# Pair slots of a ViT block: second norm folded behind two transposes, one lag more for ranks and scatters

## What is computed

```python
xn = _layernorm(x, norm1_w, norm1_b)
qkv = (xn @ qkv_w.T + qkv_b)...                  # 12 heads of 16
attn = softmax(q @ k.T * scale); o = attn @ v
x = x + (o @ proj_w.T + proj_b)
xn2 = _layernorm(x, norm2_w, norm2_b)            # the second norm
logits = xn2 @ w_gate                            # 8 experts
top_vals, top_idx = top_k(logits, 2); gates = softmax(top_vals)
h = gelu(xn2 @ W1[e] + b1[e])                    # 768 wide, for the token's two experts
x + sum over e of gate_e * (h @ W2[e] + b2[e])
```

## Time and profile before

| | us |
|---|---|
| median of 3 runs | 1150.55 (1149.22 to 1151.24) |
| the profiled execution | 1158.98 |
| its span | 1157.1 |
| PE, DVE, ACT, POOL busy in the span | 998.3, 636.4, 466.9, 565.4 |
| pair slots | about 484 to 835 |
| expert tiles | about 852 to 1112 |

### The profile page before, as it was taken

The page is one execution under the profiler, slowest core; times in us unless marked ns, Lnnn a source line. Parts: engine busy times, 40 slices in busy tenths (PEclk is TensorE's granted clock), DMA queues, the critical chain, the costliest instruction groups (busy, mean ns, idle before and its releaser), DMA issues.

```text
span 1157.1 us, 24046 instructions
## 1 busy us (share of the span) xinstructions
PE 998.3 (86%) x6992; PEld 854.6 (74%) x6993; DVE 636.4 (55%) x1649; ACT 466.9 (40%) x1172; POOL 565.4 (49%) x1094
## 2 busy tenths in 40 slices
PE   7899999999997987599888888888349999999960
PEld 4789889889975654488677776766339999999950
DVE  7477585575437787466667666665412222222216
ACT  1234323233213444345565555555114444444424
POOL 2578586676421223414666666666504444434330
PEclk9989999999988998799899999998569999999985
DMA  8564662470103300306200000000011111111118
GB/s 356 205 266 189 225 275 95 190 306 34 39 11 62 63 1 0 58 1 266 105 13 16 16 16 16 16 16 19 26 48 38 41 43 43 36 43 42 44 35 253
DMA packets 41701, 103.09 MB, mean 89 GB/s; under 512 B 7046, under 2 KB 28656, under 8 KB 38837
## 3 DMA queue, kind: packets, MB, share of 16 engines
q1 hardware_dynamic: 30085, 88.86, 22.1%
q0 software_dynamic: 5760, 9.68, 2.5%
q10 hardware_dynamic: 5808, 3.96, 1.1%
HBM read 86.30 MB, written 18.32 MB: 90 GB/s over the span
## 4 chain that ended last, share of the span: by engine, by line
PE 35%; POOLq 22%; issue 21%; POOL 7%; DVE 6%; DMA 4%; ACT 2%; DVEq 1%; SPq 1%; ACTq 0%
PE pe L1631 16%; POOLq L561 6%; POOLq L537 4%; PE pe L1640 4%; POOLq L526 2%; DMA x<-yy_d 2%; POOL xn L532 1%; POOLq L539 1%; POOLq L510 1%; POOLq L551 1%; POOL xs_d L529 1%; DVE sc L316 1%; PE pe L183 1%; DMA raw<-in_xw 1%; PE pe L184 1%
## 5 line engine op out<-in xcount | busy, mean ns | idle before, releaser
L1631 PE MATMUL pe<-wm,xm 128*128 128x193 f32 x1008 | 174.1, 331 | 1.7 <-issue 1.7
L1631 PEld LDWEIGHTS pe<-wm,xm 128*128 128x128 f32 x1008 | 168.0, 192 | 6.4 <-issue 6.4
L844 ACT ACTIVATE hT<-pe,eb 128x128 f32<-128x128 f32 x336 | 92.8, 375 | 147.6 <-PE pe L970 147.5
L983 PE MATMUL pp<-w2s,hT 128*128 x672 | 118.5, 326 | 0.0
L983 PEld LDWEIGHTS pp<-w2s,hT 128*128 128x128 f32 x672 | 107.9, 190 | 0.2
L967 PE MATMUL pe<-xsT,ew 128*128 128x128 f32 x672 | 89.4, 284 | 3.3 <-ACT xsT L834 3.3
L967 PEld LDWEIGHTS pe<-xsT,ew 128*128 128x128 f32 x672 | 81.1, 195 | 8.6 <-ACT xsT L834 4.1
L759 DVE TENSOR_TENSOR ys<-pp,b2s 128x192 f32<-128x192 f32 x56 | 20.0, 358 | 121.4 <-PE pp L983 118.5
L529 POOL DMA_INDIRECT xs_d<-xsrc,dst x64 | 65.6, 1025 | 41.7 <-issue 41.7
L557 POOL DMA_INDIRECT yy_d<-ys,yix x56 | 57.2, 1022 | 46.5 <-issue 46.5
L1355 POOL TENSOR_TENSOR sqs<-sqs,sqt 128x448 f32<-128x448 f32 x56 | 67.5, 1205 | 8.0
(11 more groups left out here) (267 smaller groups left out, 2220.3 us busy)
## 6 DMA issues: line engine op xcount, KB each, us to landing
xm<-in_xm SPq DMA_DIRECT2D x7, 2688.0 KB, 14.0
raw<-in_xwa SPq DMA_DIRECT2D x7, 1792.0 KB, 7.2
raw<-in_xwb SPq DMA_DIRECT2D x7, 1536.0 KB, 11.4
x<-in_x SPq DMA_DIRECT2D x4, 1536.0 KB, 8.6
xs<-xs_d SPq DMA_DIRECT2D x56, 96.5 KB
x<-yy_d SPq DMA_DIRECT2D x8, 672.0 KB
w1s<-in_W SPq DMA_DIRECT2D x1, 4608.0 KB
w2s<-in_W SPq DMA_DIRECT2D x1, 4608.0 KB
```

What stands on the lines that cost most here:

```text
L844: last = f(self.hT[:, u, c], pe1[:, 2 * u + c % 2, (c // 2) * ROWS:(c // 2 + 1) * ROWS], ACT.Gelu, bias=self.b1[:, u, c:c + 1])
L983: last = mm(pp[:, u, 0:D], self.hT[:, u, n], self.w2s[:, bass.ds(e, 1), n * D:(n + 1) * D].rearrange("p o d -> p (o d)"), start=(n == 0), ...
L1631: mm(y[:, 0:D + 1], cell(q, c), wm[:, q, c], start=(q + c == 0), stop=(q == 3 and c == KC - 1))
```

## The change

The second norm's weight and bias leave POOL. They are now per-partition columns: `colg` gets two more columns for the gate logits, and `n2` becomes a 128x2x2 tile for the expert tiles. They are applied by ACT where it copies transposed data out of PSUM: `xnT2` in the pair slots and `xsT` in the expert tiles, each now two Identity instructions of 128 columns (one for each half of the 192 numbers) with a scale column and a bias column, where one plain copy of 256 columns stood. POOL keeps the two statistics columns of every pair in a new tile `rn` (one more drain and copy), so that ACT can write `xsrc` two slots later from `x2`. Ranks go from lag 6 to 7, `xsrc` from 5 to 7, the scatter from 7 to 8 (40 POOL slots in place of 39), and POOL's slot ends with a drain. The values' products go to a bank of `pp`, so that the scores no longer wait for `on`. On DVE the first norm's statistics come first in a slot; the order on PE and ACT is changed as well.

```diff
-        self.n2 = sb("n2", [P, 2, D])
+        self.n2 = sb("n2", [P, 2, 2])
+        self.rn = sb("rn", [P, NP, 2])
...
-            a, b, c, d = item(0), item(4), item(3), item(7)
+            a, c, d = item(0), item(3), item(8)
...
-            if b:
-                pool.wait_ge(self.c_x, b[0] + 1)
-                g.tensor_tensor(self.xn[:, b[1]], self.xn[:, b[1]], self.n2[:, 0], ALU.mult)
             if d:
                 i, u, _ = d
-                pool.wait_ge(self.d_src, i + 2)
+                pool.wait_ge(self.d_src, i + 1)
                 pool.wait_ge(self.d_dst, i + 1)
...
-            pool.drain()
-            if d:
+                pool.drain()
                 for k in range(2):
...
-            if b:
-                g.tensor_tensor(self.xn[:, b[1]], self.xn[:, b[1]], self.n2[:, 1], ALU.add).then_inc(self.c_xn, 1)
...
-                g.tensor_scalar(st[:, 9:10], st[:, 6:7], st[:, 8:9], -1.0, ALU.mult, ALU.mult).then_inc(self.c_r, 1)
+                g.tensor_scalar(st[:, 9:10], st[:, 6:7], st[:, 8:9], -1.0, ALU.mult, ALU.mult)
+                pool.drain()
+                g.tensor_copy(self.rn[:, bass.ds(i, 1), :].rearrange("p o k -> p (o k)"), st[:, 8:10]).then_inc(self.c_r, 1)
...
-        run_slots(pool, NP, 8, slot)
+            pool.drain()
+        run_slots(pool, NP, 9, slot)
...
-            f(self.xsT[:], pt1[:, u, 0:2 * ROWS].rearrange("p (h n) -> p h n", h=2), ACT.Copy).then_inc(self.e_xT, 1)
+            for h in range(2):
+                last = f(self.xsT[:, h], pt1[:, u, h * ROWS:(h + 1) * ROWS], ACT.Identity, bias=self.n2[:, h, 1:2], scale=self.n2[:, h, 0:1])
+            last.then_inc(self.e_xT, 1)
...
+            if n7 is not None:
+                u, h = item(7)[1:]
+                act.wait_ge(self.scat[u], 32 * h)
+                f(self.xsrc[:, u, :, 0:D], self.x2[:, bass.ds(n7, 1), :].to_broadcast([P, 2, D]), ACT.Identity, bias=col(n7, 1), scale=col(n7, 0)).then_inc(self.d_src, 1)
...
-                pe.wait_ge(self.b_on, n2)
...
-                            last = mm(pe1[m * B:(m + 1) * B, 0, n * w:(n + 1) * w], self.pT[:, n, m * B:(m + 1) * B], self.vbd[:, m, n], start=True, stop=True)
+                            last = mm(pp[m * B:(m + 1) * B, 1, 256 + n * w:256 + (n + 1) * w], self.pT[:, n, m * B:(m + 1) * B], self.vbd[:, m, n], start=True, stop=True)
```

More of the change, by code:

```diff
@@ L607, in slot @@
         def slot(item):
-            n0, n1, n2, n3, n6 = (item(lag) and item(lag)[0] for lag in (0, 1, 2, 3, 6))
+            n0, n1, n2, n3, n6, n7 = (item(lag) and item(lag)[0] for lag in (0, 1, 2, 3, 6, 7))
             lg = self.lg
             dve.drain()
+            if n0 is not None:
+                v.bn_stats(self.bn[:, 0], row(hall, n0))
             if n6 is not None:
@@ L617, in slot @@
                 v.tensor_copy(lg[:], pe1[:, 3, 256:256 + E]).then_inc(self.d_lgo, 1)
+            dve.drain()
             if n0 is not None:
-                v.bn_stats(self.bn[:, 0], row(hall, n0))
-            dve.drain()
+                v.bn_aggr(st[:, 0:2], self.bn[:, 0]).then_inc(self.a_var, 1)
             if n2 is not None:
@@ L669, in slot @@
                 v.reciprocal(self.mx2[:], o[:, :, AHD:AHD + 1].rearrange("p h o -> p (h o)"))
-            dve.drain()
-            if n2 is not None:
+                dve.drain()
                 dve.wait_ge(self.c_T, n2)
@@ L776, in scalar, with row, col @@
         act.wait_ge(self.init, 2)
+        def row(t, i):
+            return t[:, bass.ds(i, 1), :].rearrange("p o d -> p (o d)")
+        def col(i, k):
+            return self.rn[:, bass.ds(i, 1), k:k + 1].rearrange("p o k -> p (o k)")
         def slot(item):
-            n0, n1, n2, n3, n4, n5, n6 = (item(lag) and item(lag)[0] for lag in (0, 1, 2, 3, 4, 5, 6))
+            n0, n1, n2, n3, n4, n5, n6, n7 = (item(lag) and item(lag)[0] for lag in (0, 1, 2, 3, 4, 5, 6, 7))
+            if n2 is not None:
+                act.wait_ge(self.b_sub, n2 + 1)
+                f(self.pm[:, :, 0:T], self.pm[:, :, 0:T], ACT.Exp, scale=AHD ** -0.5).then_inc(self.b_ex, 1)
+            if n5 is not None:
+                act.wait_ge(self.c_nT, n5 + 1)
+                for h in range(2):
+                    last = f(self.xnT2[0:H2, h], pe1[0:H2, 3, h * P:(h + 1) * P], ACT.Identity, bias=colg[:, h, 6:7], scale=colg[:, h, 5:6])
+                last.then_inc(self.d_out, 1)
             if n3 is not None:
@@ L804, in slot @@
                 f(self.xh2[:], self.x2[:, bass.ds(n0, 1), :].rearrange("p o d -> p (o d)"), ACT.Copy, scale=self.st[:, 3:4]).then_inc(self.a_xh, 1)
+            if n4 is not None:
+                act.wait_ge(self.c_r, n4 + 1)
+                f(self.xn[:, item(4)[1]], row(self.x2, n4), ACT.Identity, bias=col(n4, 1), scale=col(n4, 0)).then_inc(self.c_x, 1)
+            if n0 is not None:
                 act.wait_ge(self.a_T, n0 + 1)
@@ L872, in slot @@
         def slot(item):
-            n0, n1, n2, n3, n5, n6 = (item(lag) and item(lag)[0] for lag in (0, 1, 2, 3, 5, 6))
+            n0, n1, n2, n3, n5, n7 = (item(lag) and item(lag)[0] for lag in (0, 1, 2, 3, 5, 7))
             if n2 is not None:
@@ L924, in slot @@
                     last.then_inc(self.b_pT, 1)
-            if n5 is not None:
-                pe.wait_ge(self.d_out, n5 + 1)
-                for h in range(2):
-                    last = mm(pe1[:, 3, 256:256 + E], self.xnT2[:, h], self.wgate[:, h], start=(h == 0), stop=(h == 1))
-                last.then_inc(self.d_lg, 1)
+            if n3 is not None:
+                pe.wait_ge(self.c_out, n3 + 1)
+                mm(pe1[:, 2, 256:256 + D], self.onT[:, 0], self.wproj[:, 0], start=True, stop=False)
+                mm(pe1[:, 2, 256:256 + D], self.onT[:, 1], self.wproj[:, 1], start=False, stop=True).then_inc(self.c_proj, 1)
             if n2 is not None:
                 pe.wait_ge(self.a_v, n2 + 1)
+                if n1 is not None:
+                    pe.wait_ge(self.a_k, n1 + 1)
                 w = 2 * (AHD + 1)
```

133 lines of the change are left out of this document (60 added, 73 removed).

## The result

| | us |
|---|---|
| median before, 4 runs beside the changed kernel | 1150.89 (1149.22 to 1154.87) |
| median of the changed kernel, 4 runs | 1174.51 (1174.45 to 1175.40) |
| ratio | 1.0202 (95% interval 1.0175 to 1.0229) |
| span of the profiled execution, before and after | 1157.1 and 1172.6 |

The kernel became 23.6 us slower; the forecast was 20.9. To see whether the sum was right or only its total, I cut both traces at the same places: at the first POOL step of the first norm in each of the 32 slots (L507, now L508) and at the first matmul of each expert tile (L967, now L976).

What follows compares the result with a forecast made beforehand. POOL's own list was taken to bound the pair slots, a ring through `xsT` the expert tiles. Terms 21.3 + 4.6 - 4 - 2 + 1 = +20.9 us on 1150.55 gave 1171.5 us; eight-in-ten range 1160 to 1184.

Steps and rivals of the forecast that it cites:

- The ring of the expert tile: Expert tiles: L970, Gelus, `xsT`, L967, L970 form a 4.59 us ring, so longer `xsT` counts fully, +21.3 us over 56 tiles.
- The rival by which `xsT` is hidden: Expert tiles: PE's own list sets the tile, so `xsT` costs 4.5 us instead of 21.3; 1155 us, chance 0.08.
- The price of the pair: Expert tiles: two Identity instructions take 0.80 us where one copy took 0.42, +0.38 us a tile.
- The drain: POOL's pair slot: the drain ends 1.4 to 1.6 us after the second transfer regardless, so removing L532 gains 0.
- The rival that gives the time back: POOL's pair slot: the drain before L538 only waits for L536, slot 0.55 us shorter than forecast; 1160 us, chance 0.08.
- POOL's slot: Pair loop: POOL's own list grows by 0.22 us a slot (-0.53 to +0.52), +4.6 us over 21 slots.
- The drain and copy into `rn`: POOL's pair slot: a drain gap of 0.17 and a copy of 0.22, less 0.05 overlap, +0.34 us a slot.
- The end drain: End of POOL's slot: +0.21 us for the drain and +0.2 for register and branch work no longer covered.
- In the loop this is worth nothing: Pair loop: the new order on DVE, PE and ACT gains 0, since all these engines already wait for POOL.
- Before the loop: Slots before the loop: an earlier aggregate and freed scores give back 4 us (0 to 8).
- Slots 8 to 10 and behind slot 31: First loop slots: -2 us from POOL's wait for DVE's aggregate; after the loop: +1 us for later ranks and scatters.
- The clock: Expert tiles: rival that PE's granted clock falls from 1.00 to 0.96, +5.6 us; 1177 us, chance 0.12.

Runs made afterwards that it cites:

- split_only: Kernel before with only `xsT` written by two Identity instructions with scale and bias columns (ones and zeros); ratio 1.0243 to the kernel before.
- one_copy: Changed kernel with `xsT` as one plain copy again, norm2's weight and bias left out of the experts' input; ratio 0.9951 to the kernel before.
- no_L532: Kernel before without L532, POOL's addition of norm2's bias behind the scatter's transfers; ratio 0.9999 to the kernel before.
- sum_in_shadow: input_first with POOL's residual sum moved from the slot's end to ahead of the drain behind the transfers; ratio 0.9821 to the kernel before.
- no_L520: Kernel before without L520, POOL's multiplication by norm2's weight ahead of its two indirect transfers; ratio 1.0025 to the kernel before.
- old_order: Changed kernel with `bn_aggr` again behind the two score instructions and PE's scores again waiting for `on`; ratio 1.0269 to the kernel before.
- before_input_first: Kernel before with `xsT` of the next tile ahead of the six Gelus in ACT's expert loop; ratio 0.9932 to the kernel before.
- input_first: Changed kernel with the two `xsT` instructions of the next tile ahead of the six Gelus on ACT; ratio 0.9931 to the kernel before.
- old_order_short: sum_in_shadow without the drain ending POOL's slot, with the same two order parts undone as in old_order; ratio 0.9865 to the kernel before.

## Why the prediction was right, and where its sum was off

**The ring of the expert tile: right.** The step said that `xsT` lies on the path although ACT is idle for more than half of the time, since every link of the ring starts 0.05 to 0.13 us behind the one before. The links stand again after the change, split_only puts the loss into the kernel before, one_copy takes it out of the changed one, and the exchange on ACT breaks the ring in both. The rival by which `xsT` is hidden fell with PEld's 32.3 us of waits for `xsT` and with the tiles of 5.01 us.

**The price of the pair: 0.84 us, not 0.80.** I took L807, whose two instructions write 96 partitions; L839's write 128. Whether the partitions make the difference wasn't tried. That is 0.42 a tile in place of 0.38, and the tiles took 23.5 us more over their 55 intervals, where I had 21.3 for 56. By the Trainium skill, "ScalarE: Activation LUTs", section "What ACT_TABLE_LOAD costs", the pair was 865 ns, an estimate which I had set aside for the row; measured are 840, nearer to the page than to my row.

**The drain: right.** "So 0, and the drain before L538 gets visibly idler instead": the wait ahead of L533 is 1.34 in place of 0.79, no_L532 gains nothing, sum_in_shadow hides 0.55 us. The rival that gives the time back fell three times.

**POOL's slot: +0.30, not +0.22.** Of the terms, removing L520 gave 0.53 in the changed kernel, where nothing else took its place. The drain and copy into `rn` came to 0.43 for 0.34: from L535 to L539 it is 0.65 us (653.20 to 653.85), where L540 to L542 was 0.22. The end drain came to 0.40 (1.09 and 0.82 by turns less 0.55) for 0.41. -0.53 + 0.43 + 0.40 = +0.30, times 20 slots 6.0 us. The term that was short is the small drain: its gap is 0.22 us and not 0.17, and the last 0.05 us of the instruction ahead of it (0.27 long, L542 began 0.22 behind its start) are no longer overlapped.

**"In the loop this is worth nothing": right for the wrong reason.** I argued that all engines wait for POOL. They did, but the hand-overs can set the slot once POOL's list is shorter or the clock lower, as no_L520 shows, and old_order costs 3.3 us in the loop of the changed kernel. In the kernel before, with its old order, the -0.53 for L520 did not come at all. A term that was put at zero may carry another one: no run here separates the order from the clock.

**Before the loop: -7.0, not -4.** The order makes 2.9 of it. Another 2.1 are one slot: slot 7 takes 8.55 us even with the old order and took 10.67, since with a scatter lag of 8 it has no transfers yet. I had put this lag only behind the loop, as a cost, and not ahead of it, as the same thing the other way. The remaining 2 us lie in slots 3 to 5 (0.48, 0.48 and 0.96); slot 5 ran at a granted clock of 0.82 before and at 1.00 in old_order. I didn't trace them further.

**Slots 8 to 10 and behind slot 31: -1.5 and -2.1, for -2 and +1.** Neither sign is shown. Against before_input_first, whose pair slots are the same as before, they are +1.1 and 0.0. POOL's wait for DVE's aggregate that I counted on in two slots is not there in that execution: its slots 8 and 9 take 9.61 and 9.80 us, where they took 10.94 and 11.13. Behind slot 31 the chain to the first tile runs over the last ranks and the matmul that totals them (L955, now L964). It starts 49.4 us behind slot 31 before and 46.7 after; from there to the first tile it is 18.3 and 18.9. The last scatter ends 4.6 and 8.1 us behind that matmul, beside this chain. So the lags that I had priced at +1 didn't make the totals later: the four traces with the pair slots of the kernel before have 47.3 to 49.5, the changed kernel, input_first and one_copy 46.7 to 47.0, and old_order 48.8. With the old order the whole stage takes 68.3 and 67.9 (old_order_short), in the six traces of the changed kernel with the new one 64.9 to 66.3, so the order does count there.

**The clock: the rival fell where I had put it.** The granted clock stayed at 1.00 in the tiles, with PE busy 228.7 of 239.0 us. In the pair slots it is 0.97, but there it moves with the long slots of no_L520, old_order and old_order_short, and the prediction had no such term.

**The total.** Measured stage by stage +18.9, by the medians +23.6 with 20.1 to 26.4 as the interval. The changed kernel's profiled execution took 1174.47 us, its median is 1174.51, and it has no tile of 5.5 us; so those, worth about 5 us where they occur, don't fill the difference. It lies on the other side: the profiled execution of the kernel before took 1158.98 us, 8.1 above its median. The 29.1 and 65.6 us of before_input_first would make up 4.8 of that; that the median executions look so is likely and not shown. How much of the hit is luck hangs on it. The terms for the tiles and the loop came to 25.9 and measured 29.4. The rest was to give back 5 and gave back 10.6 in the two profiled executions, and would have given back 5.7 beside before_input_first.

## What to carry to other kernels

Before an instruction is moved to an idle engine, follow its result to the next wait: an engine busy 42% of the time can own the ring that sets the stage, and here the order of its two jobs (input for the next tile first) is worth more than the number of instructions. Work in the time that a drain spends on a transfer is free, so removing it gains nothing and moving other work there gains its full length. An order that is "worth nothing" because another list covers it has to be priced again once that list gets shorter, and a lag is counted at both ends of the pipeline. Where slots of one loop differ in length, read the granted clock slot by slot before the order is blamed, and compare more than one execution before a stage's 2 us are explained.

## What the runs showed of the hardware

- A POOL drain behind an indirect transfer let the next instruction start 1.54 to 1.61 us after the transfer's end with 0.21, 0.22 or 0.81 us of instructions in between (1.41 with none); without a transfer the same drain took 0.14 us on top of the instruction before it (552.77 to 552.91).
- A drain of POOL ahead of a slot's register and branch work costs 0.27 and 0.54 us by turns (0.40 on the mean) where a 0.59 us instruction covered that work, and 0.26 on the mean where a 0.22 us copy did.
- Two Identity instructions of 128x128 with a scale and a bias column take 0.84 us together, one copy of 128x256 takes 0.42.
- Shortening the bounding engine's list by 0.53 us a slot made the slots 0.38 us longer in no_L520, with the granted clock at 0.86 over them in place of 0.96. Slots at 1.00 took 9.04 to 9.10 us, twelve at 0.77 to 0.91 took 10.6 or 10.7, five at 0.81 took 9.03 to 9.20. The scores' matmuls took 0.42 us at the upper level of the clock and 0.71 at the lower.
